# Two-layer graph network on one core: degrees as row sums of the adjacency, and five changes of order

## What is computed

```python
A = zeros(N, N).at[src, dst].add(edge_weight)
deg = sum(A, axis=1)
dinv = where(deg > 0, deg ** -0.5, 0)
An = dinv[:, None] * A * dinv[None, :]
h = x
for l in range(2):
    h = An @ h
    h = h @ W_gcn[l] + b_gcn[l]
    h = leaky_relu(h @ W_mlp[l] + b_mlp[l], 0.01)
x = layernorm(x + h)
# second block: the same edges, unweighted, with self loops
deg1 = in-degree + 1;  dis = deg1 ** -0.5
h = relu(conv(x, W1) + b1);  h = conv(h, W2) + b2      # conv: dis * (counts^T @ (dis * x W))
out = layernorm(x + h)
```

## Time and profile before

| | |
|---|---|
| median of three executions | 327.63 us |
| the profiled execution | 327.37 us, of which the span of instructions is 325.6 us |
| TensorE (PE) busy | 306.2 us (94%), 1913 products |
| VectorE (DVE) busy | 213.5 us (66%) |
| ScalarE (ACT) busy | 132.5 us (41%) |
| GpSimd (POOL) busy | 52.7 us (16%) |
| mean granted clock of TensorE | 0.997 of 2.4 GHz |
| adjacency loop, first to last chunk | 8.9 to 77.8 us |

### The profile page before, as it was taken

How to read it: one execution, slowest core, us unless ns; L and a number is a source line. 1 busy time by engine, 2 the same in 40 slices (tenths; PEclk the granted TensorE clock), 3 DMA queues, 4 the chain that set the end, 5 groups by cost and what they waited for, 6 DMA issues and landing times.

```text
span 325.6 us, 4903 instructions
## 1 busy us (share of the span) xinstructions
PE 306.2 (94%) x1913; PEld 251.6 (77%) x1913; DVE 213.5 (66%) x382; ACT 132.5 (41%) x279; POOL 52.7 (16%) x54
## 2 busy tenths in 40 slices
PE   1968999999899999999999999999999989999992
PEld 1857876887688888888888888888888868888881
DVE  6998999723735425255543878897989784225664
ACT  3538798645544411134432033336914673220000
POOL 2100000002003990320000001021000940001111
PEclk9999999999999999999999999999999999999998
DMA  6282300200020000000710000004000300000121
GB/s 210 73 274 85 98 2 2 66 2 2 3 64 1 2 0 4 0 3 1 256 68 0 0 0 2 0 2 163 3 0 10 120 2 0 0 4 34 65 96 66
DMA packets 11455, 14.52 MB, mean 45 GB/s; under 512 B 4514, under 2 KB 4898, under 8 KB 11428
## 3 DMA queue, kind: packets, MB, share of 16 engines
q1 hardware_dynamic: 11428, 14.15, 13.3%
HBM read 12.02 MB, written 2.12 MB: 43 GB/s over the span
## 4 chain that ended last, share of the span: by engine, by line
PE 87%; DVE 8%; issue 2%; ACT 1%; DMA 1%; POOLq 0%; POOL 0%; SPq 0%; ACTq 0%
PE psum L796 67%; PE psum L1032 8%; PE psum L854 6%; PE psum L782 3%; DVE hot L1212 2%; PE psum L901 1%; DVE sel L1204 1%; DVE hot L1207 1%; PE psum L838 1%; DVE w_low L1566 1%; DVE wm_low L1297 1%; DVE wgt_low L1284 1%; DMA src_i<-in_src 1%; PE psum L860 1%; ACT hot L559 0%
## 5 line engine op out<-in xcount | busy, mean ns | idle before, releaser
L854 PEld LDWEIGHTS psum<-hot,sel 128*128 128x128 bf16 x512 | 28.7, 102 | 7.0 <-issue 6.6
L854 PE MATMUL psum<-hot,sel 128*128 128x96 bf16 x512 | 32.5, 215 | 1.4 <-DVE hot L1212 1.2
L545 POOL TENSOR_TENSOR small<-small 128x1 f32<-128x1 f32 x16 | 10.8, 677 | 131.8 <-DVE small L1451 131.8
L1284 DVE SCALAR_TENSOR_TENSOR y_low<-psum,small,y_high 128x512 fp32r<-128x512 f32 x16 | 11.9, 749 | 24.8 <-ACT y_high L559 24.8
L796 PE MATMUL psum<-at_high,x_high 128*128 128x512 f32 x64 | 25.8, 403 | 0.6 <-DVE x_low L1372 0.6
L796 PE MATMUL psum<-at_low,x_high 128*128 128x512 f32 x64 | 25.1, 392 | 0.0
L796 PE MATMUL psum<-at_high,x_low 128*128 128x512 f32 x64 | 24.9, 390 | 0.0
L796 PE MATMUL psum<-y_high,at_high 128*128 128x512 f32 x64 | 24.9, 389 | 0.0
L796 PE MATMUL psum<-y_high,at_low 128*128 128x512 f32 x64 | 24.9, 389 | 0.0
L796 PE MATMUL psum<-y_low,at_high 128*128 128x512 f32 x64 | 24.9, 389 | 0.0
L796 PE MATMUL psum<-y_high,cnt 128*128 128x512 f32 x64 | 24.9, 389 | 0.0
(11 more groups left out here) (215 smaller groups left out, 790.5 us busy)
## 6 DMA issues: line engine op xcount, KB each, us to landing
wg_raw<-in_L_gnn_W_gcn SPq DMA_DIRECT2D x2, 1024.0 KB, 5.6
x_raw<-in_x SPq DMA_DIRECT2D x8, 256.0 KB, 2.6
xs<-in_x SPq DMA_DIRECT2D x1, 2048.0 KB, 9.4
w_raw<-in_L_gnn_W SPq DMA_DIRECT2D x2, 1024.0 KB, 5.5
out<-xs SPq DMA_DIRECT2D x8, 256.0 KB, 2.0
wm_raw<-in_L_gnn_W_mlp SPq DMA_DIRECT2D x1, 1024.0 KB, 8.3
wm_next<-in_L_gnn_W_mlp SPq DMA_DIRECT2D x1, 1024.0 KB, 9.5
col_scale<-scales SPq DMA_DIRECT2D x2, 512.0 KB, 5.9
```

Of the source, the lines that this page charges most:

```text
L545: pool.tensor_tensor(r[:, 1:2], r[:, 0:1], power[:, 0:1], ALU.pow).then_inc(rstd_ready, 1)
L854: ins = pe.matmul(sums[1 if k == 0 else 0], stationary, moving, start=False, stop=False, skip_group_check=True)
L1284: dve.scalar_tensor_tensor(out=dest, in0=tile, scalar=scale, in1=high.bitcast(F32), op0=ALU.mult, op1=ALU.subtract).then_inc(low_made[name ...
```

## The change

- **Degrees.** The products `degree`, the table `hw`, `hi_f`'s turn and its part of `tables`, and bank 4's role are gone. VectorE instead sums the rows of `adj` in pieces (`tensor_reduce` over whole column ranges, between the last `add_ends`), then the last two regions' own columns and their ends apart, then the eight partial sums.
- **Order 1.** ScalarE's share of batch 4 comes whole after chunk 27, behind the evacuation of region 3.
- **Order 2.** The last group of boundaries is cut in two, (17, 17) and (18, 19), and ScalarE copies regions 18 and 19 together, all of `adj` before any of `cnt` (`evacuate_last`).
- **Order 3.** After `dinv` both engines begin with `x` 0, then `at` 0, then `wc1` 3. TensorE turns two blocks before `g1_a` instead of three.
- **Order 4.** `w2_low` comes in pairs after rows 5 and 6 of h3.
- **Order 5.** GpSimd's bias adds wait for the end of h3's products.
- Fillers use four banks, 4 to 7, and the end of a batch is told by `region_done` where a region ends with it.

```diff
-    BOUNDARIES = [(1, 4), (5, 8), (9, 12), (13, 14), (15, 16), (17, 19)]
+    BOUNDARIES = [(1, 4), (5, 8), (9, 12), (13, 14), (15, 16), (17, 17), (18, 19)]
-    SHARED = {4: {21: 6, 27: 10}, 5: {40: 16}, 7: {66: 8, 73: 8}}
+    SHARED = {4: {27: 16}, 5: {40: 16}, 7: {66: 8, 73: 8}}
+    IN_FRONT = {27: 6}
-        FILL, WIDE = (5, 6, 7), (4, 5, 6, 7)
+        FILL = WIDE = (4, 5, 6, 7)
+        def whole_columns(n):
+            c0 = REGION * (BOUNDARIES[n - 1][1] + 1) if n else 0
+            return slice(c0, min(N, REGION * (BOUNDARIES[n][1] + 1)))
...
-            pool.wait_ge(c_low, 2 * KD)
+            pool.wait_ge(done["h3"], 2 * KD)
...
+            def evacuate_last():
...
+                for kind, sums in enumerate((adj, cnt)):
+                    slots = [psum[:, 2 * (r % 2) + kind, :].rearrange("p (h d) -> p h d", d=PITCH) for r in range(2)]
+                    act.wait_ge(region_done, NR - 1)
+                    copy(sums[:, :, d18:d18 + PITCH], slots[0]).then_inc(evacuated, 1)
+                    act.wait_ge(region_done, NR)
+                    copy(sums[:, :, d19 + WINDOW:], slots[1][:, :, WINDOW:N - d19]).then_inc(evacuated, 1)
+                    copy(ends_at(kind, NR - 1, NR - 1), slots[1][:, :, 0:WINDOW].unsqueeze(2)).then_inc(evacuated, 1)
...
             for c in stops:
-                if c in closing:
+                if c == closing[NR - 1]:
+                    evacuate_last()
+                elif c in closing and c != closing[NR - 2]:
                     evacuate(closing.index(c))
+                if c in IN_FRONT:
+                    scale_columns(4, 0, IN_FRONT[c])
...
+            upper_x(0)
             upper_at("at", 0, 0)
-            for j in range(NB):
+            upper_fill("wc1", KD - 1)
+            for j in range(1, NB):
+                upper_at("at", 0, j)
                 upper_x(j)
-                if j + 1 < NB:
-                    upper_at("at", 0, j + 1)
...
-                if c >= LATE_HW:
-                    ins = degree(c)
-                    if c + 1 in batch_of:
-                        ins.then_inc(batch_used, 1)
-                    if c == CH - 1:
-                        ins.then_inc(loop_done, 1)
-                if c == LATE_HW - 1:
-                    pe.wait_ge(hw_made, 1)
-                    for k in range(LATE_HW):
-                        ins = degree(k)
...
-            for j in range(3):
+            for j in range(2):
                 turn_adjacency("at", 0, j)
...
-                if j + 3 < NB:
-                    turn_adjacency("at", 0, j + 3)
+                for k in range(j + 3 if j else 2, min(j + 4, NB)):
+                    turn_adjacency("at", 0, k)
...
-            dve.wait_ge(spill_ready, 1)
-            make_hw()
...
-            make(9, 0)
-            make(9, 1)
+            make_all(9)
             add_ends(2)
-            for k in range(2, 5):
-                make(9, k)
             lower_fill("wc1", 0)
             lower_fill("wc1", 1)
             uncovered = dve.value_load(flags[0:1, 0:1], min_val=0, max_val=1)
+            def sum_rows(n):
+                dve.wait_ge(head_added, 2 * n + 1)
+                dve.tensor_reduce(deg_parts[:, :, n:n + 1], adj[:, :, whole_columns(n)], AX.X, ALU.add)\
+                    .then_inc(deg_summed, 1)
+
+            sum_rows(0)
             add_ends(3)
+            sum_rows(1)
+            lower_fill("wc1", 2)
+            sum_rows(2)
             add_ends(4)
-            lower_fill("wc1", 2)
-            dve.wait_ge(loop_done, 1)
-            step(dve.tensor_reduce(deg, bank("deg")[:, 0:3 * NB].rearrange("p (a h) -> p h a", a=3), AX.X, ALU.add))
-            step(dve.tensor_scalar(deg_pos, deg, 0.0, None, ALU.is_gt))
-            dve.tensor_scalar(deg_safe, deg, 1.2e-38, None, ALU.max).then_inc(deg_ready, 1)
+            sum_rows(3)
+            sum_rows(4)
             add_ends(5)
+            sum_rows(5)
+            dve.wait_ge(evacuated, copies(NR - 3) + 2)
+            dve.tensor_reduce(deg_parts[:, :, LAST:LAST + 1], adj[:, :, whole_columns(LAST)], AX.X, ALU.add)\
+                .then_inc(deg_summed, 1)
+            dve.wait_ge(evacuated, copies(NR - 3) + 3)
+            dve.tensor_reduce(deg_parts[:, :, LAST + 1:LAST + 2], ends_at(0, *BOUNDARIES[LAST]), AX.XY, ALU.add)\
+                .then_inc(deg_summed, 1)
+            dve.wait_ge(deg_summed, LAST + 2)
+            dve.tensor_reduce(deg, deg_parts[:], AX.X, ALU.add).then_inc(deg_made, 1)
+            def degrees():
+                dve.wait_ge(deg_made, 1)
+                dve.tensor_scalar(deg_safe, deg, 1.2e-38, None, ALU.max).then_inc(deg_ready, 1)
+                dve.tensor_scalar(deg_pos, deg, 0.0, None, ALU.is_gt).then_inc(deg_made, 1)
...
-                lower_fill("wc1", 3)
+                lower_x(0)
                 lower_at("at", 0, 0)
-                for j in range(NB):
+                lower_fill("wc1", KD - 1)
+                for j in range(1, NB):
+                    lower_at("at", 0, j)
                     lower_x(j)
...
-                    if n == 2 * KD - 2:
-                        lower_w(w2_high_made, w2_low_made, w2_raw, w2_high, w2_low)
+                    if KD < n < KD + 3:
+                        lower_w(w2_high_made, w2_low_made, w2_raw, w2_high, w2_low, range(2 * (n - KD - 1), 2 * (n - KD)))
...
             with dve.If(uncovered < 1):
+                degrees()
+                add_ends(LAST)
                 after_adjacency(True)
```

More of the change, by code:

```diff
@@ L332, in first_of, with batch_is_used @@
             return BATCHES[n][0] if n < 3 else 0
+        ends_of = [b + n - 1 for b, n in BATCHES]
+        def batch_is_used(eng, n):
+            if ends_of[n] in closing:
+                eng.wait_ge(region_done, closing.index(ends_of[n]) + 1)
+            else:
+                eng.wait_ge(batch_used, sum(1 for c in ends_of[:n + 1] if c not in closing))
+        def whole_columns(n):
+            c0 = REGION * (BOUNDARIES[n - 1][1] + 1) if n else 0
+            return slice(c0, min(N, REGION * (BOUNDARIES[n][1] + 1)))
         def copies(r):
@@ L634, in _ @@
                     if c in parts:
-                        scale_columns(n, sum(v for k, v in parts.items() if k < c), parts[c])
+                        done_before = IN_FRONT.get(c, 0)
+                        scale_columns(n, sum(v for k, v in parts.items() if k < c) + done_before,
+                                      parts[c] - done_before)
                 if c == 3:
@@ L801, in _ @@
             pe.wait_ge(ident_ready, 1)
-            pe.wait_ge(edge_ready, 2)
-            turn(bank("prep", 0), [lo_f[:], hi_f[:]]).then_inc(prep_done, 1)
+            pe.wait_ge(edge_ready, 1)
+            turn(bank("prep", 0), [lo_f[:]]).then_inc(prep_done, 1)
             pe.wait_ge(w_in, 16)
@@ L856, in chunk @@
                 return ins
-            def degree(c):
-                buf, own = where(c)
-                return pe.matmul(bank("deg")[:, 0:3 * NB].rearrange("p (a h) -> p a h", a=3), sel[buf][:, own, :],
-                                 hw[:, :, c, :],
-                                 start=(c == 0), stop=(c == CH - 1), skip_group_check=True)
             def filler(name, i, k0, k1):
@@ L910, in _ @@
             load_offsets(0)
-            LATE_HW = 35
             for c in range(CH):
@@ L1206, in make @@
                 elif k == 1:
-                    ins = dve.tensor_tensor(sums(0), counting(COLS), column(2, COLS), ALU.is_equal)
+                    ins = dve.tensor_tensor(sums(0), counting(COLS), column(1, COLS), ALU.is_equal)
                 else:
@@ L1211, in make @@
                     dve.wait_ge(made, sets_made(n - 1) + 2)
[L1212 removed]
+                    ins = dve.tensor_tensor(sums(k - 1), sums(0), column(k, COLS), ALU.mult)
                 ins.then_inc(made, 1)
[L1215 to L1225 removed]
             def check_windows():
@@ L1561, in after_adjacency, with lower_w @@
                     lower_sum(j, s2_low[:, j, :], s2_sum[:, j, :], s2_high[:, j, :], s2_high_made, s2_low_made)
-                def lower_w(high_sem, low_sem, raw, high, low):
-                    for k in range(KD):
+                def lower_w(high_sem, low_sem, raw, high, low, ks=range(KD)):
+                    for k in ks:
                         dve.wait_ge(high_sem, k + 1)
@@ L1689, in _ @@
                     dve.wait_ge(gen_step, 5 + (hf + 1) * (NB + 2))
+                dve.tensor_reduce(deg, adj[:], AX.X, ALU.add).then_inc(gen_step, 1)
+                dve.wait_ge(gen_step, 5 + 2 * (NB + 2) + 1)
+                degrees()
                 after_adjacency(False)
```

79 lines of the change are left out of this document (32 added, 47 removed).

## The result

Eight executions of the changed kernel against eight of the one before: 326.58 us (326.23 to 327.77) against 327.49 us (327.35 to 327.76), ratio 0.9978, 95% interval [0.9968, 0.9987]. It is faster, by 0.9 us, where 2.65 was forecast. The profiled execution took 326.23 us.

What follows compares the result with a forecast made beforehand. It took TensorE to bound the kernel (87% of the chain of waits), with the degrees' way deciding g1_a's start. 1.45 + 1.2 = 2.65 us off 327.37 gave 324.7 profiled, 325.0 at the median; range 323.8 to 326.9.

Steps and rivals of the forecast that it cites:

- (a): Loop, clear before chunk 31: the stop of 1.24 us goes, as region 3's evacuation precedes batch 4's scalings; gain 1.2 us.
- (b): Loop: the block of 35 degree products on TensorE, 30.53 to 31.41 us, goes; gain 0.88 us.
- (c): Loop: the 93 other degree products go at 0.031 us each; gain 2.9 us, of which 2.4 by chunk 112.
- (d): Loop: busy ScalarE makes TensorE wait at the clears at chunks 57 and 83; 0.6 us taken off the gain.
- the loop: TensorE's chunks: region 16 ends at chunk 112 3.9 us earlier, and the loop near 73.7 instead of 77.8 us.
- The row sums: VectorE's reductions at 1.04 ns an element, 9.3 us together: deg_safe ends at 77.57 us, before at 78.61.
- From the degrees to g1_a: After deg_safe: dinv at 79.54 us, then 2.2 us instead of 3.03 in the new order; g1_a at 81.75, 1.83 earlier.
- y3: Between h3 and y3: w_low in pairs and GpSimd's adds moved behind h3 remove TensorE's wait; gain 1.2 us.
- The third turn: Inside g1_a: the turn moved behind its first 12 products costs about 0.4 us back.
- A: The forecast itself, whole kernel: 325.0 us, of its own 324.2 to 325.7; chance 0.58.
- B: Rival, before g1_a: TensorE's 4.1 us standstill drops the clock to half, 1.5 us lost, 326.5 us; chance 0.18.
- Left: 1.45: At g1_a: what remains of its 1.83 us earlier start after about 0.4 us back for the third turn.

Runs made afterwards that it cites:

- the order repairs alone: The kernel before with all the changes of order, degrees still made by the 128 degree products and the table: 325.11 us, ratio 0.9915.
- the fastest kernels: The changed kernel with wcb_low 2 behind deg_pos, three turns before g1_a and nine zero products: 322.93 us; with the old order after dinv as well: 322.85 us.

## Why the prediction was wrong

By its own steps:

- **(a), (b), (c), (d), the loop.** Right as a sum: chunk 112 comes 3.89 us earlier (72.21 to 68.32), 3.9 forecast. Chunk 32 starts 1.2 us earlier (30.00 to 28.81), with no stop before batch 4, as (a) has it. Against the kernel that keeps the degree products, the block of 35 is 0.91 us (0.88 forecast), and from chunk 35 to 112 the changed kernel is 1.92 us faster (forecast: 2.45 less the 0.6 of (d), 1.85). In detail (d) is 0.3, the two waits named above; TensorE's timeline of the changed kernel has the one before chunk 83:

```profile
56.72 0.34 PE L867 MATMUL psum<-ramp,none 128*128 128x192 bf16 x2 [0.19 <-ACT cnt L571]
```

  With it 78 products are 2.2 us, 0.029 each, where I took 0.031. So (d) was twice too large and (c) somewhat, in opposite directions.
- **The row sums.** Right: 1.88 us for 1664 elements, where 0.15 + 1664 x 0.00104 makes 1.88; deg_safe at 77.55 where 77.57 stood.
- **From the degrees to g1_a.** Right in its end (81.91 for 81.75; from dinv 2.31 us for 2.2) and unproven in its reason. The 0.83 us between 2.2 and 3.03 I gave to the new order alone. With the short loop the old one reaches `g1_a` just as early, since `wc1` 3 is done before dinv. With the long loop and the new order (the order repairs alone) it is 2.31 us as well, from 79.49 to 81.80. So the shorter loop is enough for the gain without the new order, and the two are not to be counted twice.
- **y3.** Right: 22.99 to 21.79 us, 1.20. The pairs alone don't do it: with GpSimd's adds early only 0.46 of it is left. What the late adds would give without the pairs, no run shows.
- **The third turn.** Right: 0.4 us (50.08 against 49.68).
- **The choice between A and B** is the step that failed. In "Left: 1.45" and "1.45 + 1.2 = 2.65" the price of the clock after the pause stands at nothing; it was 1.36 us in the profiled execution. Rival B had the mechanism, the place and the size: a pause of 4.1 us (4.35), the clock at half, 1.5 us lost (1.36), 326.5 us (326.58). I gave it 0.18 with one sentence, "the gap is hardly longer than what the end shows". That sentence was itself an argument for B: the end showed a fall 3.6 us after the last product, and a forecast pause of 4.1 us is longer than that. It was also one reading taken as a fixed one: over the thirteen traces of this case the clock falls 2.4 us (the kernel with the six scalings in their old place) to 5.2 us (the changed kernel, and the one with the h3 repair undone) after the kernel's last product. And the pause was 3.3, not four, times the longest stop in the loop, 1.24 us. The forecast for the kernel was A's sum, 2.65; B's was 1.15, and 0.9 came. The measured 326.58 lies in the stated range, which had been drawn to take in B.

How sound the rest of the sum was, the traces show better than the times. Without the 1.36 of the clock the changed kernel's span would be 2.54 us shorter than before, for 2.65. But the changed kernel with its pause filled, the direct test, came to 325.61, 2.0 us below the kernel before, and the rest of the 2.65 is only in part accounted for there. That the order repairs alone gave 2.5 us (327.63 to 325.11) is no proof of the sum: there (a) and the new order brought deg_safe and `g1_a` to the same times, and (b) and (c) were not in it. The row sums are what made the pause; against the kernel that keeps the products they made the degrees known earlier, by 1.45 us, only after `wc1` 2 was moved behind them.

**Open:** why the clock comes back after 3.4 us in one execution and 6.8 in another; and how long a pause is safe. A pause of 1.16 us kept the clock in all five executions, 1.85 in four of five, 2.75 in none of five, 4.35 in none of the 19 of the changed kernel. One or two of each have a trace; the others are judged by time and mean clock.

## What to carry to other kernels

When work is taken from the engine that bounds the kernel, ask first whether what it waits for comes earlier as well; if not, the saved time is a pause, and a pause of TensorE can cost clock on top (here 1.4 to 2.7 us, after pauses of 2.75 to 4.35). Fill such a pause with work that has to be done anyway (here the third turn, 0.4 us), and what is left with products of zeros (here nine to sixteen of them, for 1.4 us of clock), or leave the "wasteful" products in.

A wait on an engine in front of a long series of work (`wc1` 2, 2.12 us idle) is worth a look before the work is made shorter: moving it was worth 1.45 us at the degrees, as much as the clock. And an order repaired for the old lengths should be tried again with the new ones; in the fastest kernels the new order after dinv was worth nothing.

## What the runs showed of the hardware that was not expected

- The granted clock can fall after TensorE has gone back to work: 0.9 us after, in the second trace of the changed kernel, and 1.5 us after, with `wc1` 2 behind the degrees.
- It came back after 3.4 us in three traces and after 6.8 us in one, with TensorE busy from the start of `g1_a` on; the loss was 1.4 and twice 1.6 us, and 2.7 us.
- After the kernel's last product the clock fell 2.4 to 5.2 us later. The window of the shortest of these, whose last product ends at 317.12:

```profile
318.00:320.00 2.00, 0.00 (x0) 0.00 (x0) 1.27 (x4) 0.00 (x0) 0.55 (x1) 0.89 0.09 34
```

- Products with a zero operand kept the clock up: in the six traces of the kernels with nine, eleven or sixteen of them it is full until after the last product, and the mean was 0.994 to 0.999 in all their 25 executions.
- A reduction of float32 on VectorE costs 0.15 us and 1.04 ns an element from 192 (0.34 us) to 2080 elements (2.32 us), also over strided pieces.
